# Transposing the activations of layers 2 and 3 of a graph network by DMA in place of TensorE

## The reference

```python
edge_index = stack([src, dst])                       # 16384 edges, 1024 nodes
x = layernorm(x + L0(x))    # h = x@W + b; out = sum_i w_i * adj^i h, i = 0..3; relu
x = layernorm(x + L1(x))    # segment_sum(x[src], dst) @ W.T + b
x = layernorm(x + L2(x))    # x@wc + mean over neighbours of (x@wn) + bias
x = layernorm(x + L3(x))    # 8 heads of graph attention, head width 64
```

## Time and profile before

| | us |
|---|---|
| median of 3 runs (lowest to highest) | 409.59 (409.47 to 409.86) |
| profiled execution | 408.27 |
| its span, first to last instruction | 406.4 |
| TensorE busy | 376.9 |
| VectorE, ScalarE, GpSimd busy | 278.5, 244.4, 93.4 |

### The profile page before, as it was taken

The page is one execution under the profiler, slowest core; times in us unless marked ns, Lnnn a source line. Parts: engine busy times, 40 slices in busy tenths (PEclk is TensorE's granted clock), DMA queues, the critical chain, the costliest instruction groups (busy, mean ns, idle before and its releaser), DMA issues.

```text
span 406.4 us, 8206 instructions
## 1 busy us (share of the span) xinstructions
PE 376.9 (93%) x2832; PEld 222.8 (55%) x2832; DVE 278.5 (69%) x603; ACT 244.4 (60%) x406; POOL 93.4 (23%) x87
## 2 busy tenths in 40 slices
PE   1798888999999999999999999999899999999990
PEld 1244436544444444444445454445456889999990
DVE  7778998838995775206633222555599588999984
ACT  9789785575813155202665221247774999999534
POOL 4520000029930167300764000133100000012110
PEclk9999999999999999999999999999999999999996
DMA  6950005005000000000000000000001213220005
GB/s 192 389 159 2 1 0 202 9 0 203 6 0 2 0 0 3 2 0 2 1 0 2 0 0 3 0 0 0 2 1 33 76 53 105 79 81 2 3 3 210
DMA packets 10040, 18.54 MB, mean 46 GB/s; under 512 B 2128, under 2 KB 2320, under 8 KB 10000
## 3 DMA queue, kind: packets, MB, share of 16 engines
q1 hardware_dynamic: 9136, 14.86, 10.7%
q10 hardware_dynamic: 864, 3.15, 2.2%
HBM read 15.87 MB, written 2.13 MB: 44 GB/s over the span
## 4 chain that ended last, share of the span: by engine, by line
PE 77%; DVE 13%; issue 4%; DVEq 2%; ACT 2%; ACTq 0%
PE ps L744 18%; PE ps L1120 13%; PE ps L969 7%; PE ps L1013 7%; PE ps L925 7%; PE ps L907 7%; PE ps L1061 7%; DVE c L1274 4%; PE ps L897 3%; PE ps L777 3%; PE ps L886 3%; PE ps L917 2%; DVE big L1510 2%; DVE adj L1255 1%; PE ps L798 1%
## 5 line engine op out<-in xcount | busy, mean ns | idle before, releaser
L744 PE MATMUL ps<-big,xTs 128*128 128x512 f16 x384 | 85.5, 379 | 1.7 <-ACT xTs L442 1.5
L744 PEld LDWEIGHTS ps<-big,xTs 128*128 128x128 f16 (+1 forms) x384 | 36.8, 98 | 44.3 <-issue 2.4
L653 ACT ACTIVATE big<-big,uvt 128x1024 bf16<-128x1024 f32 x55 | 59.0, 1148 | 0.0
L414 POOL TENSOR_TENSOR big<-xcur,big x24 | 27.7, 1155 | 123.9 <-ACT xcur L535 123.5
L534 ACT ACTIVATE big<-xcur,nmr,rstd (+1 forms) x24 | 19.5, 813 | 36.8 <-DVE nmr L1380 36.8
L777 PE MATMUL ps<-big,xTs 128*128 128x512 f32 x64 | 34.7, 638 | 0.0
L442 ACT ACTIVATE xTs<-ps 128x512 f16<-128x512 f32 (+2 forms) x24 | 20.1, 878 | 20.4 <-PE ps L969 17.7
L442 ACT ACTIVATE big<-ps 128x512 f16<-128x512 f32 (+2 forms) x17 | 9.7, 573 | 34.2 <-PE ps L744 24.6
L1061 PE MATMUL ps<-big,cst 128*128 128x260 f16 x256 | 29.8, 275 | 0.0
L384 POOL TENSOR_TENSOR big<-xTs,big 128x2048 f16<-128x2048 f32 x4 | 16.2, 4076 | 58.8 <-ACT big L442 58.8
L798 PE MATMUL ps<-adj,cts 128*128 128x80 f16 (+31 forms) x128 | 21.1, 268 | 9.3 <-DVE c L1274 5.0
(11 more groups left out here) (208 smaller groups left out, 677.4 us busy)
## 6 DMA issues: line engine op xcount, KB each, us to landing
big<-u_rows ACTq DMA_DIRECT2D x6, 512.0 KB, 3.7
xTs<-in_xT SPq DMA_DIRECT2D x2, 1024.0 KB, 9.2
xcur<-in_x SPq DMA_DIRECT2D x1, 2048.0 KB, 17.3
out<-xcur SPq DMA_DIRECT2D x8, 256.0 KB, 2.4
big<-in_W SPq DMA_DIRECT2D x1, 1024.0 KB, 5.9
cts<-in_W3T SPq DMA_DIRECT2D x1, 1024.0 KB, 12.9
xTs<-in_W1T SPq DMA_DIRECT2D x1, 1024.0 KB, 5.2
xTs<-in_wc SPq DMA_DIRECT2D x1, 1024.0 KB, 8.1
```

Of the source, the lines that this page charges most:

```text
L653: act.activation(above[:, a % AHEAD, :], uf[:, h % 2], ACT.Relu, scale=BIG, bias=vb[:, j, h:h + 1]).then_inc(S["above_in"], 1)
L744: return mm(bank, lhs(k)[a], rhs(k)[b], start=start and k == 0 and n == 0, stop=stop and k == KT - 1 and n == 2)
```

## The change

TensorE's transposes and ScalarE's evictions are removed. SP issues for each tile of the two layers eight transposing transfers from SBUF to SBUF, one for each 128x128 block, after `x_lo`. They raise one of two semaphores, by the tile's parity, by 16 each, and a tile's transfers wait until those of the tile before the last one have all landed. TensorE waits in `turned` for all eight transfers of its tile (8 x 16 = 128). ScalarE's orders by hand become plain loops, as the evictions that they were woven around are gone; VectorE's `products_in2(0)` and `(1)` move behind the norm loop.

```diff
+TURNED = 8 * 16
@@ sync engine, after the weights
+            for layer in range(1, 3):
+                for t in range(NT):
+                    name = ("xT_even", "xT_odd")[t % 2]
+                    n = (layer - 1) * NT + t
+                    sp.wait_ge(S["x_lo"], layer * NT + t + 1)
+                    if n >= 2:
+                        sp.wait_ge(S[name], n // 2 * TURNED)
+                    for v in range(2):
+                        for k in range(KT):
+                            sp.dma_start(xTs[:, v, k, t * P:(t + 1) * P], cur[:, 1, v, t, k * P:(k + 1) * P],
+                                         transpose=True).then_inc(S[name], 16)
@@ ScalarE
-            def xT_evict(layer, t, i):
-                act.wait_ge(S["xT_done"], t + ((layer - 1) * NT + 1))
-                copy(xTs[:, :, :, bass.ds(t * P, P)].rearrange("p v k n -> p (v k) n"),
-                     bank16(i).rearrange("p (a n) -> p a n", n=P)).then_inc(S["xT_in2"], 1)
...
+            with act.Fori(0, NT // 2) as r:
+                for i in range(2):
+                    norm(1, r * 2 + i, i)
+            with act.Fori(0, NT // 2) as r:
+                for i in range(2):
+                    z_hi(r * 2 + i, i)
+            with act.Fori(0, NT // 2) as r:
+                for i in range(2):
+                    norm(2, r * 2 + i, i)
+            act.activation(std[:, 0:1], epsc[:], ACT.Exp).then_inc(S["warm"], 1)
+            act.wait_ge(S["warm"], 2)
+            exps(0, 0)
+            y_upper(0, 0)
+            with act.Fori(0, NT // 2 - 1) as r:
+                for i in (1, 0):
+                    t = r * 2 + (2 - i)
+                    exps(t, i)
+                    y_upper(t, i)
@@ TensorE
-            def transposes(layer, t, i):
-
-                pe.wait_ge(S["x_lo"], t + (layer * NT + 1))
-                for v in range(2):
-                    for k in range(KT):
-                        a = v * KT + k
-                        ins = pe.transpose(bank16(i)[:, a * P:(a + 1) * P], cur[:, 1, v, t, k * P:(k + 1) * P], id16[:])
-                ins.then_inc(S["xT_done"], 1)
...
+            def per_tile(layer, products):
 
                 pe.wait_ge(S["y_ready"], layer * NT + 6)
-                products(0, 0)
-                with pe.Fori(0, NT // 2 - 2) as r:
+                products(0, 0, 0)
+                with pe.Fori(0, NT // 2 - 1) as r:
                     for i in (1, 0):
-                        t = r * 2 + (2 - i)
-                        transposes(layer, t + 1, 1 - i)
-                        products(t, i)
...
+                        products(r * 2 + (2 - i), i, r + (1 - i))
+
+            def turned(layer, i, pair):
+                pe.wait_ge(S["xT_odd" if i else "xT_even"], pair * TURNED + ((layer - 1) * NT // 2 + 1) * TURNED)
...
-            transposes(1, 0, 0)
-            transposes(1, 1, 1)
             product1(NT - 1)
...
-                    transposes(2, 0, 0)
-                    transposes(2, 1, 1)
                     tile(NT - 1, parts)
...
-            def products2(t, i):
+            def products2(t, i, pair):
+                turned(1, i, pair)
...
-            def products3(t, i):
+            def products3(t, i, pair):
+                turned(2, i, pair)
@@ VectorE
-            norm_loop(1, total1, products_in2)
-
-            products_in2(1, 1)
-            with dve.Fori(1, NT // 2) as r:
+            norm_loop(1, total1)
+
+            with dve.Fori(0, NT // 2) as r:
```

More of the change, by code:

```diff
@@ L936, in _ @@
             step(NT - 1, False)
-            def per_tile(layer, products, before_last=None):
+            def per_tile(layer, products):
                 pe.wait_ge(S["y_ready"], layer * NT + 6)
-                products(0, 0)
-                with pe.Fori(0, NT // 2 - 2) as r:
+                products(0, 0, 0)
+                with pe.Fori(0, NT // 2 - 1) as r:
                     for i in (1, 0):
-                        t = r * 2 + (2 - i)
-                        transposes(layer, t + 1, 1 - i)
-                        products(t, i)
[L947 to L953, removed]
+                        products(r * 2 + (2 - i), i, r + (1 - i))
+            def turned(layer, i, pair):
+                pe.wait_ge(S["xT_odd" if i else "xT_even"], pair * TURNED + ((layer - 1) * NT // 2 + 1) * TURNED)
             def product(layer, name, bank, done, free, n, t):
-                pe.wait_ge(S["xT_in2"], t + ((layer - 1) * NT + 1))
                 pe.wait_ge(S[free], n)
@@ L997, in _ @@
                 product1(t)
-            transposes(1, 0, 0)
-            transposes(1, 1, 1)
             product1(NT - 1)
             def gather2():
-                pe.wait_ge(S["xT_in2"], NT)
                 pe.wait_ge(S["y_ready"], 2 * NT)
@@ L1035, in _ @@
             per_tile(1, products2)
-            products2(NT - 1, 1)
+            products2(NT - 1, 1, NT // 2 - 1)
             pe.wait_ge(S["alpha_in"], NT + 2)
             gather2()
-            def products3(t, i):
+            def products3(t, i, pair):
+                turned(2, i, pair)
                 product(2, "W3", 4 + i, "wx_done", "wx_in", t + 1, t)
@@ L1048, in scores_rows @@
             def scores_rows():
-                pe.wait_ge(S["xT_in2"], 2 * NT)
+                for i in range(2):
+                    turned(2, i, NT // 2 - 1)
                 pe.wait_ge(S["y_ready"], 3 * NT)
@@ L1072, in _ @@
             per_tile(2, products3)
-            products3(NT - 1, 1)
+            products3(NT - 1, 1, NT // 2 - 1)
             pad(7)
```

## The result

The changed kernel takes 487.51 us (median of 4 runs, 487.27 to 488.75) against 409.53 us before on the same chip: ratio 1.192, interval 1.188 to 1.195. The profiled execution has a span of 486.8 us, 80.4 more than before; it is the longest of the four, the spans of the others are 485.4 to 485.7 us. The forecast was 492 to 493 us.

What follows compares the result with a forecast made beforehand. TensorE was taken as the bound, VectorE for the last tiles. 74.6 us of late transfers plus 8.4 for the clock, 83.0 on 408.27, gave 491.3; with 1.3 for the median, 492 to 493 us, range 402 to 560.

Steps and rivals of the forecast that it cites:

- The direction and the bound: Products2 and products3: TensorE would wait for transfers, gather 34 us late, end 74.6 us late; slower had chance 0.77.
- The pitch: Distance p between successive transposing transfers on SP's queue, taken as 1.3 us, the flight of a 32 KB transfer without issue.
- the formula 126p - 89.2: Loss in us if both product stages stall, p being the time between successive transfers; 74.6 us late at 1.3.
- The ratio of 1.23: Skill's 631 against 512 sequencer cycles; on a 0.57 us issue it gave an estimate of 0.70 us.
- The clock: TensorE at 1.2 GHz after pauses in products2 and products3; the last products cost 5.2 + 3.2 = 8.4 us more.
- The tail: From line 1497's last tile to the end: no change in the length, 97 us.
- The sum as a whole: Whole kernel: 74.6 us late plus 8.4 us for lower TensorE speed, 83.0 us on the profiled 408.27 us.
- The gain that could be had: Removed transposes and evictions: 3.6 us up to products2's end, 0.9 in the gather, 1.8 in products3, 6.3 in all.
- The third term: Products3: ScalarE's evictions no longer hold up TensorE's product at the start; 1.8 us given in all.
- the break-even: Time between successive transfers at which the loss is zero, 0.71 us; a wash there had chance 0.03.

Runs made afterwards that it cites:

- e3: Changed kernel with transfers for products2 alone, products3 having its TensorE transposes and evictions back: 445.17 us, ratio 1.087 to the kernel before.
- e5: Changed kernel with SP waiting after each of the 128 transfers until it has landed: 612.52 us, ratio 1.498 to the kernel before.
- e1: Changed kernel with two transposing transfers of 128x512 for a tile in place of eight of 128x128: 403.98 us, ratio 0.988 to the kernel before.
- e2: Changed kernel with the same transfers made without turning, so activations aren't transposed: 406.40 us, ratio 0.995 to the kernel before.
- e4: Changed kernel with idle matmuls ahead of TensorE's wait for each tile but tile 0: 484.89 us, ratio 1.186 to the kernel before.
- e6: Changed kernel with four transposing transfers of 128x256 for a tile in place of eight: 406.42 us, ratio 0.994 to the kernel before.

## Why the prediction came out

**The direction and the bound.** Right: the stages changed from TensorE to the transfers, each by 63 pitches (e3 has one alone, 36.9 us), and the gather and the dense sums are late by it.

**The pitch.** 1.3 us was taken and 1.275 measured; the formula 126p - 89.2 gives 71.5 us with it, in place of 74.6. But the reason given for 1.3 was wrong. It was the flight of a 32 KB transfer, with transfers running one after another. In fact SP is held by the issue: 1.10 us even with nothing in flight (e5), 1.27 us for four times the data (e1). The next issue does run while the transfer ahead hasn't landed (2.3 us to landing at a pitch of 1.275), but from the end of an issue to its landing it is only 1.1 us, so whether two turning transfers would hold each other up in the DMA engines no run shows; it never came to that. That the number agreed is luck. The difference matters for what one does next: from serial transfers one would expect the loss to stay with larger ones, while a price by instruction goes away with them, and e1 shows that it does.

The Trainium skill's page DMA: Bandwidth & Descriptors, Rules for kernel authors, has it that transfers under 64 KB are mostly overhead. The trace agrees for the 32 KB transfers: SP is held for 1.23 us by each while the DMA engines are busy for 0.12 of the time. That the line lies at 64 KB no run here shows, and at 128 KB the issue was still 1.27 us. The Trainium skill's sentence in Advanced Engine Details and Errata, X-Bar Transpose (TRN2), that turning transfers are as fast as regular ones, is not what decides here: per instruction the turning one took twice the issue (1.23 against 0.60 us in e2). The ratio of 1.23, from which the prediction estimated 0.70 us, was too small as well: measured it is 2.05.

**The clock.** The direction was right, the size twice too large: 8.4 us in the sum, while the last products show 7.90 - 5.35 = 2.55 (5.35 is one at full clock behind a pause) and 4.22 - 2.76 = 1.5 us, 4.0 in all, as in e4. I had let a product run at the 1.2 GHz level throughout. After its pause a product starts at about 0.43 us a matmul and is back at 0.216 about halfway: the last one of products2, from 279.64 to 287.54, has a granted clock of 0.50 up to 284.6 and of 1.00 from 285.1 on. So the page has 7 as the lowest tenth of the clock in products2 and 6 in products3, where 5 or 6 was forecast. That the pauses are the cause is shown by e4. How long one must be is not: a pause of 2.02 us in products2 was followed by a clock of 1.00, one of 2.08 us in e6 by a stretch of 0.65 (298.3 to 302.5).

**The rest of the 79.3 us** until the last tile is taken: 71.5 + 4.0 = 75.5; a product behind a pause takes 5.35 us even at full clock where the sum has 5.18, 0.2; landing at 2.3 in place of 1.8 us adds 1.0 over two stages, the first issue at 195.97 in place of 195.66 adds 0.3, and two issues of 1.88 and 2.55 us, one in each stage, add 2.0. That is 79.0.

**The tail.** "None in the length from line 1497's last tile to the end" was wrong by 1.2 us: 486.8 - 388.5 = 98.3 in place of 97.1. Before, the first 16 dense matmuls ran while VectorE was catching up; now VectorE has caught up and they stand ahead of the transpose of uvt, which starts at 390.70 although its operand is there at 389.5. The other runs bear this out: where the last tile waited for its transfers this length is 98.2 to 98.6 us (e2, e4, e5, e6), and in e1, where VectorE is the one behind, 97.2.

**The sum as a whole.** 83.0 us were forecast on the profiled execution and 80.4 measured. The pitch and the clock were 3.1 and 4.4 us too dear, and 3.5 us of smaller terms and 1.2 in the tail were put at nothing. The forecast then added 1.3 us, as the median was above the profiled time before; now it is 1.2 below it.

**The gain that could be had.** 6.3 us in the sum; e1 has 4.7 us at the last tile. Up to the gather 3.4 us came (250.39 to 247.03 by the chain, 3.6 in the sum, and the earlier end of the linear layer is in it), in the gather 0.9. The third term, 1.8 us for ScalarE's evictions in products3, was mis-sized: some 0.5 is left for it. The wait of 1.5 us for an eviction hid another: with it gone TensorE waits 1.18 us for VectorE's line 1460 ahead of the same tile. From the first uvt to the last tile's line 1460 (1497 before) it is 21.57 us in e1, and before 309.26 - 287.71 = 21.55.

**What stays open.** Why issuing a turning transfer holds SP twice as long as an ordinary one; how much the clock costs in a usual execution (4.0 us in the two traces, some 2.2 us by the medians); and what it would have brought to issue from a second engine's queue, which no run tried.

## What to carry to other kernels

Price a transfer by what its issue costs the queue, not by its bytes or by how idle the DMA engines look: here 128 KB cost as much issue as 32 KB, and eight instructions for a tile against two are 487.5 against 404.0 us. When work moves from a full engine to an idle one, multiply the new instruction's issue by its count in a stage and set that against the time which the stage had; the break-even (0.71 us here) tells what has to be known before anything else. If the count is what loses, widen the instruction before giving up the idea: e1 is the version to keep, 1.2% faster than before.

## What was not expected of the hardware

A turning transfer of SBUF to SBUF cost SP 1.10 us alone and 1.23 us in a row, at 128x128, 128x256 (1.25) and 128x512 (1.27) alike; the same blocks without turning cost 0.60 us, itself more than the 0.37 us of a 1 MB load. And in products2 the clock of TensorE alternated with the pauses: behind 5 us of waiting a tile took 8.2 us, its end left a pause of only 2 us, and the next tile took 5.35 us again. The same stage in e3 didn't alternate; there tile after tile took 7.04 us behind some 3 us.
